# A four-layer GNN kernel: a quarter of each block's turn-back goes from TensorE to VectorE

## The reference

```
for l in range(NUM_LAYERS):
    m = x @ weight[l]
    agg = segment_sum(m[src], dst, num_segments=n_nodes)
    x = gru_cell(agg, x, w_ih, w_hh, b_ih, b_hh)
...
r = sigmoid(i_r + h_r); z = sigmoid(i_z + h_z)
n = tanh(i_n + r * h_n)
x_new = (1 - z) * n + z * h
...
out = layernorm(x + (x_layer4 + x), axis=-1)
```

## Time and profile before

| | |
|---|---|
| median of three timed runs | 2384.56 us |
| span of the profiled execution, first to last instruction | 2340.9 us |
| launch and end around the span (median less span) | 43.7 us |
| PE busy | 2222.1 us (95%) |
| DVE busy | 2192.5 us (94%) |
| ACT busy | 1845.3 us (79%) |
| POOL busy | 1742.1 us (74%) |
| DMA, mean | 155 GB/s |

### The profile page before, as it was taken

The page is one execution under the profiler, slowest core; times in us unless marked ns, Lnnn a source line. Parts: engine busy times, 40 slices in busy tenths (PEclk is TensorE's granted clock), DMA queues, the critical chain, the costliest instruction groups (busy, mean ns, idle before and its releaser), DMA issues.

```text
span 2340.9 us, 49545 instructions
## 1 busy us (share of the span) xinstructions
PE 2222.1 (95%) x11698; PEld 1887.8 (81%) x11698; DVE 2192.5 (94%) x4410; ACT 1845.3 (79%) x3483; POOL 1742.1 (74%) x1652
## 2 busy tenths in 40 slices
PE   1899999999999999999989999999989999999996
PEld 1788888888878888888878888888877777878775
DVE  7899999999979999999969999999969999999998
ACT  1588888888768888888857888888856888888887
POOL 3788888888577777777657777777748888888884
PEclk7899999999999999999999999999999999999998
DMA  2355555555545666666545665666644555555554
GB/s 57 98 159 160 158 161 159 159 160 158 158 133 167 173 172 173 170 174 173 169 123 167 174 174 169 172 173 172 174 130 116 157 156 156 156 155 154 154 153 118
DMA packets 277063, 362.44 MB, mean 155 GB/s; under 512 B 107754, under 2 KB 186586, under 8 KB 276980
## 3 DMA queue, kind: packets, MB, share of 16 engines
q1 hardware_dynamic: 238196, 309.20, 43.7%
q0 software_dynamic: 38784, 52.30, 10.6%
HBM read 208.71 MB, written 179.20 MB: 166 GB/s over the span
## 4 chain that ended last, share of the span: by engine, by line
PE 65%; DVE 19%; issue 10%; ACT 3%; DMA 1%; POOL 1%; DVEq 1%; ACTq 0%; SPq 0%; POOLq 0%
PE pZ L818 17%; PE pR L818 17%; PE pHN L818 8%; PE pA L806 8%; PE pO L890 5%; PE pA L818 4%; PE pIN L818 4%; DVE bn L1387 3%; DVE diff L1356 2%; DVE aggT L1326 2%; DVE y_rows L1380 2%; DVE diff L1362 2%; PE pH L767 2%; DVE narg L1352 2%; POOL gath L664 1%
## 5 line engine op out<-in xcount | busy, mean ns | idle before, releaser
L664 POOL DMA_INDIRECT gath<-state,idx x900 | 931.6, 1035 | 264.0 <-issue 254.0
L641 POOL TENSOR_TENSOR h_lo<-hT,h_hi 128x500 fp32r<-128x500 f32 (+1 forms) x400 | 377.8, 945 | 191.8 <-ACT h_hi L1009 156.2
L664 POOL DMA_INDIRECT gath<-in_x_dram,idx x300 | 346.1, 1154 | 105.0 <-issue 75.4
L1039 ACT ACTIVATE rg<-pR,bsum 128x500 f32<-128x500 f32 x400 | 269.7, 674 | 112.6 <-PE pR L818 97.5
L1345 DVE SCALAR_TENSOR_TENSOR narg<-pHN,bhh,rg 128x500 f32<-128x500 f32 x400 | 293.4, 733 | 41.0 <-ACT rg L1039 38.1
L1317 DVE TENSOR_TENSOR a_lo<-aggT,a_hi 128x500 fp32r<-128x500 f32 x396 | 273.7, 691 | 0.3
L1021 ACT CAST sel<-sel 128x504 fp32r (+1 forms) x400 | 245.7, 615 | 31.1 <-DVE flag_i L1301 30.5
L1362 DVE TENSOR_TENSOR diff<-pZ,diff 128x500 f32<-128x500 f32 x400 | 268.3, 671 | 0.6
L1326 DVE TENSOR_TENSOR aggT<-pA,hT 128x500 f32<-128x500 f32 x396 | 264.6, 668 | 1.9 <-PE pA L806 1.8
L1047 ACT ACTIVATE pZ<-pZ,bsum 128x500 f32<-128x500 f32 x400 | 256.2, 641 | 0.0
L1043 ACT ACTIVATE pIN<-narg,bih 128x500 f32<-128x500 f32 x200 | 136.5, 683 | 133.5 <-DVE narg L1352 131.1
(11 more groups left out here) (205 smaller groups left out, 6367.9 us busy)
## 6 DMA issues: line engine op xcount, KB each, us to landing
columns<-newT SPq DMA_DIRECT2D x300, 250.0 KB, 2.4
hT<-columns SPq DMA_DIRECT2D x300, 250.0 KB, 2.8
state<-o_rows SPq DMA_DIRECT2D x300, 224.0 KB
x_rows<-in_x_dram SPq DMA_DIRECT2D x200, 224.0 KB
out_dram<-o_rows SPq DMA_DIRECT2D x91, 224.0 KB
gath<-state,idx POOLq DMA_INDIRECT x900, 2.5
state<-o_rows SPq DMA_DIRECT2D x300, 26.0 KB
idx<-edge_src SPq DMA_DIRECT2D x395, 1.5 KB
```

Of the source, the lines that this page charges most:

```text
L641: nc.gpsimd.tensor_tensor(part_of(h_lo, u)[:, cols], hT[:, u % RING, cols], part_of(h_hi, u)[:, cols].bitcast(F32), ALU.subtract).then_inc ...
L664: pool.indirect_dma_start(out=gath[:, u % RING, j, :], out_offset=None, in_=states[l], in_offset=bass.IndirectOffsetOnAxis(ap=idx[:, u % R ...
L1039: nc.scalar.activation(rg[:, :], pR[:, 0:COLS], ACT.Sigmoid, bias=bsum[:, 0:1]).then_inc(s_r, 1)
```

## The change

- `turn_back` does three transposes in place of four in layers 0 to 2. VectorE turns the last quarter: `turn_quarter(b-1)` stands in its order right behind `n_argument(b)` and is one 128 x 128 transpose instruction, which turns each 32 x 32 square where it stands. `newT` gets four more columns (zeros) so that the quarter is 128 wide.
- `rows_out` copies 384 columns in place of 512.
- SP stores rows of 1.5 KB (`store_turned`, two DMAs), and ahead of them four DMAs (`store_squares`), each of 32 partitions, with 4 runs of 128 bytes per partition: 512 runs of 128 bytes a block. They wait for `s_sq`, and for the squares of the block before to have landed (`s_sqst`). The next layer's first gather waits for `s_sqst` too.
- `HALF` is 350 in place of 250: in layers 1 and 2 GpSimd makes 350 columns of low h and VectorE 150.
- `select` is one comparison of 504 columns with a broadcast operand in place of three of 168 (layer 0).

```
-HALF = COLS // 2
+HALF = 350
+NPITCH = COLS + 4
+TURNED = (RPP - 1) * D
+SQUARE = 32
...
+    def squares_of(t, b, g):
+        v = bass.AP(t.tensor, (RPP - 1) * D + g * SQUARE,
+                    [[BLK * D, NB], [RPP * D, SQUARE], [SQUARE * RPP * D, P // SQUARE], [1, SQUARE]])
+        return v[bass.ds(b, 1), :, :, :].rearrange("b j c i -> (b j) c i")
...
+            def store_squares(l, b, u, first):
+                sp.wait_ge(s_sq, l * NB + b + 1)
+                sp.nop(nofuse=True)
+                if not first:
+                    sp.wait_ge(s_sqst, 64 * (l * NB + b))
+                    sp.nop(nofuse=True)
+                for g in range(P // SQUARE):
+                    sp.dma_start(squares_of(states[l + 1], b, g),
+                                 o_rows[g * SQUARE:(g + 1) * SQUARE, u % RING, TURNED:RPP * D].rearrange("p (c i) -> p c i", i=SQUARE)
+                                 ).then_inc(s_sqst, 16)
...
                         if l < L - 1:
                             if exists_before(i, u, 2):
-                                store(l, *after(i, u, -2)[:2])
+                                store_squares(l, *after(i, u, -2)[:2], l == 0 and isinstance(i, int) and i == 0 and u == 2)
+                                store_turned(l, *after(i, u, -2)[:2])
...
                     if l < L - 1:
-                        store(l, NB - 2, UNROLL - 2)
+                        store_squares(l, NB - 2, UNROLL - 2, False)
+                        store_turned(l, NB - 2, UNROLL - 2)
                         store_columns(l, NB - 1, UNROLL - 1)
-                        store(l, NB - 1, UNROLL - 1)
+                        store_squares(l, NB - 1, UNROLL - 1, False)
+                        store_turned(l, NB - 1, UNROLL - 1)
...
                             for v in range(RING):
                                 pool.wait_ge(s_store[v], 32 * TURNS * l)
+                            pool.wait_ge(s_sqst, 64 * NB * l)
...
-                for k in range(RPP):
+                for k in range(quarters):
                     last = nc.tensor.transpose(bank[0:ROWS, k * D:(k + 1) * D], newT[:, u % RING, k * CP:k * CP + ROWS],
                                                ident[:, :])
...
+            def select(b):
+                v.tensor_tensor(sel8[:, bass.ds(b, 1), :].rearrange("p o (j c) -> p (o j) c", j=TILES),
+                                node_of_col[:, :].rearrange("p (j c) -> p j c", j=TILES),
+                                edge_dl[:, :, bass.ds(b, 1)].to_broadcast([P, TILES, SELW // TILES]),
+                                ALU.is_equal).then_inc(s_sel8, 1)
...
+            def turn_quarter(l, b, u):
+                g = l * NB + b
+                if not (isinstance(b, int) and l == 0 and b < RING):
+                    dve.wait_ge(s_sqst, 64 * (g - RING + 1))
+                dve.wait_ge(s_new, g + 1)
+                v.transpose(o_rows[:, u % RING, TURNED:RPP * D],
+                            newT[:, u % RING, (RPP - 1) * CP:(RPP - 1) * CP + P]).then_inc(s_sq, 1)
...
                         n_argument(l, b, u)
+                        if not final and exists_before(i, u, 1):
+                            turn_quarter(l, *after(i, u, -1)[:2])
```

More of the change, by code:

```diff
@@ L465, in store_columns @@
                 sp.nop(nofuse=True)
-                sp.dma_start(columns_of(columns[l + 1], b), newT[:, u % RING, :]).then_inc(s_cstore[u % RING], 16)
+                sp.dma_start(columns_of(columns[l + 1], b), newT[:, u % RING, 0:COLS]).then_inc(s_cstore[u % RING], 16)
             def store(l, b, u, in_place=False):
@@ L664, in gather @@
                     pool.indirect_dma_start(
-                        out=gath[:, u % RING, j, :], out_offset=None, in_=states[l],
+                        out=gath[:, u % RING, j, :], out_offset=None, in_=states[l][0:N, :],
                         in_offset=bass.IndirectOffsetOnAxis(ap=idx[:, u % RING, j:j + 1], axis=0),
@@ L705, in edge_row @@
                         pool.nop(nofuse=True)
[L706 removed]
+                        for frm, at, to in ((states[l][0:N, :], e_src, e_rows), (edge_sum, e_dst, e_old)):
                             pool.indirect_dma_start(out=to[:, :], out_offset=None, in_=frm,
@@ L875, in z_on_sums, with turn_back @@
                 product(l, u, pZ[:, 0:COLS], 1, ("in",), False, True).then_inc(s_Z, 1)
-            def turn_back(l, b, u, start, added=None):
+            def turn_back(l, b, u, start, added=None, quarters=RPP):
                 g = l * NB + b
@@ L1052, in rows_out @@
                     act.wait_ge(s_store[u % RING], 32 * stored)
-                nc.scalar.copy(o_rows[:, u % RING, :], pO[0:ROWS, 0:RPP * D]).then_inc(s_o, 1)
+                nc.scalar.copy(o_rows[0:ROWS, u % RING, 0:cols], pO[0:ROWS, 0:cols]).then_inc(s_o, 1)
             def normalise(u, stored, shifted, part):
@@ L1290, in _ @@
             assert steps[0] == V_TABLES
[L1292 to L1299, removed]
+            def select(b):
[3 more added lines that the diff above has]
+                                ALU.is_equal).then_inc(s_sel8, 1)
+            select(0)
             dve.wait_ge(s_flag, 1)
@@ L1432, in step @@
                             if l == 0:
-                                for j in range(TILES):
-                                    select(1, 1, j)
+                                select(1)
                             first_aggregate(l, 0, l == 0)
@@ L1442, in step @@
                                 for c in range(2, RAMP):
-                                    for j in range(TILES):
-                                        select(c, c, j)
+                                    select(c)
                         added = final and exists_before(i, u, ROWLAG)
@@ L1472, in step @@
                         if l == 0 and exists(i, u, RAMP) and not ramp:
-                            for j in range(TILES):
-                                select(*after(i, u, RAMP)[:2], j)
+                            select(after(i, u, RAMP)[0])
                         difference(l, b, u)
@@ L1500, in step @@
                         if l == 0 and ramp:
-                            for j in range(TILES):
-                                select(RAMP + u, RAMP + u, j)
+                            select(RAMP + u)
                         if last:
@@ L1506, in step @@
                                 low_h(*coming[:3])
+                            if not final:
+                                turn_quarter(l, b, u)
                     blocks(dve, step)
```

44 lines of the change are left out of this document (30 added, 14 removed).

## The result

The changed kernel takes 2715.32 us (2705.06 to 2720.02, four runs) against 2383.93 (2379.89 to 2386.33, four runs): a ratio of 1.1384, 95% interval 1.1363 to 1.1405. The forecast was 2365 with a range up to 2440; even rival 1, which named the right engine, said 2455. Of all runs here one, a run of e1 of 2748.94 us at a granted clock of 0.744, was in a slower state of the chip and is left out of its ratio.

What follows compares the result with a forecast made beforehand. TensorE was taken to bound layer 0, TensorE and VectorE nearly level in layers 1 and 2. Gains of 19.4 us (layers 1, 2) and 10 (layer 0), less 10 between layers, gave 2365 us; range 2355 to 2440.

Steps and rivals of the forecast that it cites:

- rival 1: SP becomes the bound at 0.50 us a DMA: blocks 0.22 us longer in layers 1 and 2, 2455 us; chance 0.27.
- T: The new 128-column transpose instruction on VectorE, taken as 0.20 us a block.
- low_h: VectorE's low part of h in layers 1 and 2: from 250 to 150 columns, 0.10 us less a block.
- GpSimd's 350 columns: GpSimd's longer instruction: from 694 ns to at most 972, covered by its idle time, no effect.
- the ring: VectorE's closed chain through ScalarE's tanh and into the next block, layers 1 and 2: from 5.24 to 5.14 us a block.
- Rival 3: VectorE's transpose runs at half speed, 0.33 us: most of the gain lost, 2390 us; chance 0.05.
- rival 4: DMA engines saturate on the short runs: no gain in pace, 2395 us or above; chance 0.05.
- the squares cost 4 x 0.42 + 0.24 = 1.92 us: SP's added work per block: four DMAs at 0.42 us and 0.24 for the waits; SP just keeps up.
- 1.98 free: SP's waiting time per block in layer 1 after the shorter block, taken as room for the squares: 1.98 us.
- My 0.24 for the two waits: On SP, the two waits added per block with the squares' DMAs, taken as 0.24 us together.
- the 2.08 us of waits: SP's waits per block in layer 1 of the first profile, 1.40 + 0.68 us, set against the squares' cost.
- Layer ends: Between layers: last rows start 3.3 us later, three times, +10 us; TensorE idles 4.5 us before the first edge sum.

Runs made afterwards that it cites:

- e1: Changed kernel without the stores of the squares, SP storing whole 2 KB rows in two DMAs; 2362.42 us, 0.9845 of the kernel before.
- e2: Changed kernel with the four extra DMAs as 512-byte runs, one per partition, in place of four of 128 bytes; 2729.61 us, 1.140 of the kernel before.
- e8: Kernel before with 16 already met waits a block added on SP in layers 0 to 2, no DMA added; 2539.54 us, 1.0638.
- e6: Changed kernel with two DMAs of 64 partitions x 512 bytes for the squares' bytes in place of four; 2525.89 us, 1.0581 of the kernel before.
- e7: Complete changed kernel with two of the four squares' DMAs issued by ScalarE ahead of the tanh; 2468.78 us, 1.0341 of the kernel before.
- e3: Changed kernel with SP's loop over five blocks in place of ten, ten more blocks a layer written out; 2671.6 us, 1.1149 of the kernel before.
- e9: Kernel before, unchanged, run and profiled once more for its trace; 2393.03 us.
- e5: Changed kernel with one DMA of 128 partitions x 512 bytes for the squares' bytes in place of four; 2358.82 us, 0.988 of the kernel before.
- e4: Kernel before with 18 empty instructions a block on SP in layers 0 to 2, no DMA added; 2396.38 us, 1.0005.

## Why the prediction was wrong, point by point

*The computing side was right.* T was 0.22 us for 0.20, `low_h` 0.10 us less, GpSimd's 350 columns 889 ns for at most 972, the ring 5.12 us for 5.14 (e1). Rival 3 falls, and with e2 rival 4.

*The term that failed is "the squares cost 4 x 0.42 + 0.24 = 1.92 us" on SP, against 1.98 free.* It was wrong in both parts. The cost measured 2.30 us, the upper end of my own bounds: four squares at 0.51 us each, not 0.42. I averaged pairs from the quiet end of a layer with the pair from a full queue; only the second kind is what a block of layer 1 sees. SP's work became 5.39 us, 2.30 more than 3.09 for the rest, where I had 5.24 - 2.08 + 1.92 = 5.08, and that alone passes 5.14: it would have given rival 1, with a block about 0.15 us longer than in the kernel before. My 0.24 for the two waits held (0.25 with the arithmetic beside them), though a met wait by itself is 0.06 us and not 0.16 (e8).

*The free time was smaller too, and this was the larger error.* I took the 2.08 us of waits as slack. SP has pauses of about 0.7 us that this profile doesn't show. They take 5.29 - 3.16 - 1.74 = 0.4 us a block in the kernel before run again (3.16 is its work, 5.24 less 2.08), and some 0.96 us in the kernel after, which also stands 0.22 us a block at its loop's turns, a term the prediction didn't have at all. While SP waits for others, a pause is hidden in the wait. Once SP is the bound, each adds to the block: 5.39 + 0.96 + 0.22 + 0.05 = 6.62. So rival 1 named the right engine and the right direction, with a chance of 0.27, but its block was 0.22 us longer where layer 1 lost 1.07; it said +70 us, and +331 were measured. Its mechanism, issue time over free time, is not enough either: e6 with 4.96 us of work in a block and e8 with 4.02 are slow, though the other engines need more than 5.

*Layer ends.* The last `pO` of layer 0 and the first gather lie 651.26 and 656.02 us in the kernel before run again, 4.8 us apart, and 754.60 and 761.84 after, 7.2 apart: 2.5 us later for my 3.3. TensorE's last wait before the first edge sum was 2.26 us for the 4.5 forecast. Three times 2.5 is 7 us of the 331.

*What is shown and what is not.* Shown: the time is lost on SP (e1, e7, e8, and the waits of the other engines for SP's loads), not in the DMA engines or run length (e2, e8), and issue time alone doesn't explain it, since e6 is slow with 4.96 us of work in a block. In the trace of the kernel after the loss lies in the looped blocks; those written out have the same DMAs and next to no pauses. Argued: that the address arithmetic or the loop is what brings the pauses. No run writes all of SP's blocks out, and e8 has some pauses (between 2 and 9 in each written-out part) where no address is computed. The fetch of the longer loop's code is no large part by e3: 13.5 us in the same blocks. Open: what a pause is. The kernel before has some (e9), no added DMA is needed for more (e8), and with as few instruction packets as before they stay (e3). Why the execution that the first profile caught had none is as open; that SP's free time was read from just that one was bad luck.

## What to carry to other kernels

A queue's waiting time in one profile is not slack to be spent to the last tenth: here some 2 us of waits a block carried one more DMA (e5), but not two (e6). Take the queue's free time from more than one profile. Price a DMA by the row where it follows close on others, count its address arithmetic and its waits, and where the sum comes within a microsecond of the free time, expect the queue to become the bound; the bound then costs far more than the excess, since whatever the waits had hidden comes on top. Look at looped and written-out blocks apart: here the same stores cost 4.56 us a block in one and 6.62 in the other. And when a transpose saves 0.11 us on a compute engine but needs four stores on the queue that issues everything, compare the two first.

## What the runs showed of the hardware that was not expected

- SP stands still for about 0.7 us at a time on single small instructions (0.03 to 0.06 us elsewhere), without waiting for an engine: 0.4 us a block in the kernel before run again, 0.95 (e6) and 0.96 us (after) where it is busy. Nearly all of it is in looped blocks (445 against 5 in the kernel after), and none on other engines (e9).
- Where SP's loop of ten blocks is longer, it stands 2.5 to 4.1 us at each turn, with 163 to 166 instruction packets on q14 (after, e2, e8); with 51 to 60 packets (before, e3, e6) no turn in the middle of layers 0 to 2 takes over 0.75 us.
- A wait that is already met costs SP 0.06 us (16 of them 0.91 us in a quiet block, e8); empty instructions cost nothing that can be measured and don't appear (e4).
- The four squares' block takes 5.39 us on SP with computed addresses and 4.49 with fixed ones (columns stores at 1376.82 and 1381.31 in the kernel after).
- 115,200 fewer packets, in runs of 512 bytes in place of 128, changed nothing (1.140 against 1.1384).
- One 128 x 128 transpose in 32 x 32 squares of 4-byte elements costs VectorE 0.22 us from start to start, close to the 0.20 of the four instructions of 128 columns.
- Two profiles of the same kernel differ where a layer starts. The windows from 680 to 700 us, the profile before and then e9 (columns as in the earlier trace rows):

```profile
680.00:700.00 20.00, 20.00 (x105) 17.31 (x104) 17.64 (x30) 14.38 (x26) 16.80 (x18) 1.00 0.62 171
```

```profile
680.00:700.00 20.00, 15.79 (x69) 13.75 (x69) 13.65 (x23) 11.25 (x20) 10.75 (x12) 0.75 0.38 99
```

The granted clock lies between its two levels, 0.75 as a mean, in the second and is full in the first; layers 1 and 2 took 541.7 and 539.9 us there and 559.4 and 558.9 in e9.
